# A four-layer vision tower on one core: runs of two to four unread matrix products taken out of the norms and the attentions

## The reference, cut to what matters

```python
h = tokens(x)
h = h + L0_attn(layernorm(h)); h = h + L0_ffn(layernorm(h))   # 16 heads, 16 experts, top 4
h = h + L1_attn(layernorm(h)); h = h + L1_ffn(layernorm(h))   # 2 heads, 8 experts, top 2
h = h + L2_attn(layernorm(h)); h = h + L2_ffn(layernorm(h))   # mla + a shared and 7 routed experts, top 2
h = h + L3_attn(layernorm(h)); h = h + L3_ffn(layernorm(h))   # attends across images; 8 experts, top 2
```

## Time and profile before

| what | us |
|---|---|
| runs: median, lowest, highest of 3 | 851.51, 849.39, 854.37 |
| the profiled execution's own time | 857.64 |
| its span, from the first to the last instruction | 855.5 |
| PE busy | 742.4 (87% of the span), 5946 records |
| DVE busy | 393.4 (46%) |
| POOL busy | 333.6 (39%) |
| ACT busy | 221.2 (26%) |
| mean share of the DMA engines' time, all queues | 44% |

### The profile page before, as it was taken

The page is one execution under the profiler, slowest core; times in us unless marked ns, Lnnn a source line. Parts: engine busy times, 40 slices in busy tenths (PEclk is TensorE's granted clock), DMA queues, the critical chain, the costliest instruction groups (busy, mean ns, idle before and its releaser), DMA issues. The chain is left out here.

```text
span 855.5 us, 16310 instructions
## 1 busy us (share of the span) xinstructions
PE 742.4 (87%) x5946; PEld 657.4 (77%) x5946; DVE 393.4 (46%) x1093; ACT 221.2 (26%) x588; POOL 333.6 (39%) x399
## 2 busy tenths in 40 slices
PE   6897898799999788899997897798999878879997
PEld 4785688688888677899986686577888754779996
DVE  3745967545433465411132864475431337532211
ACT  1021410254445032123201410142234025111120
POOL 2336541456664131244323423521354278243211
PEclk9897997899999999799998898798999988989999
DMA  9303005588885750787524101200486630255603
GB/s 366 162 7 49 8 2 176 182 246 236 241 239 160 246 178 1 265 269 233 180 76 98 13 2 38 22 3 31 113 270 191 271 52 11 69 198 215 233 17 101
DMA packets 79203, 116.94 MB, mean 137 GB/s; under 512 B 44566, under 2 KB 58071, under 8 KB 77207
## 3 DMA queue, kind: packets, MB, share of 16 engines
q1 hardware_dynamic: 66741, 88.46, 33.4%
q0 software_dynamic: 7968, 20.20, 7.9%
q10 hardware_dynamic: 4418, 7.25, 2.3%
HBM read 99.29 MB, written 16.60 MB: 135 GB/s over the span
## 5 line engine op out<-in xcount | busy, mean ns | idle before, releaser
L280 PE MATMUL ps<-const_sb 128*128 128x128 f32 x910 | 131.3, 303 | 0.0
L280 PEld LDWEIGHTS ps<-const_sb 128*128 128x128 f32 x910 | 124.6, 218 | 1.3 <-issue 0.5
L1840 PE MATMUL ps<-l0e_xg_fm,l0e_ring 128*128 128x128 f32 x544 | 72.7, 277 | 6.8 <-ACT l0e_up_sb L1924 3.1
L1840 PEld LDWEIGHTS ps<-l0e_xg_fm,l0e_ring 128*128 128x128 f32 x544 | 67.6, 191 | 12.8 <-issue 7.5
L922 PE MATMUL ps<-x_fm,w_sb 128*128 128x296 f32 x208 | 54.3, 413 | 0.0
L308 POOL TENSOR_TENSOR norm_r<-norm_ve,const_sb 128x2 f32<-128x2 f32 (+1 forms) x27 | 19.5, 724 | 88.3 <-DVE norm_ve L301 64.0
L1840 PE MATMUL ps<-l1e_xg_fm,l1e_ring 128*128 128x128 f32 (+1 forms) x408 | 50.8, 275 | 1.1 <-ACT l1e_xg_fm L1901 0.6
L1840 PEld LDWEIGHTS ps<-l1e_xg_fm,l1e_ring 128*128 128x128 f32 (+1 forms) x408 | 48.2, 182 | 2.5 <-issue 1.7
L1741 POOL DMA_INDIRECT l0e_y_scratch<-l0e_y_tm,l0e_rows_u x34 | 35.9, 1057 | 33.9 <-ACT l0e_y_tm L1948 29.9
L922 PEld LDWEIGHTS ps<-x_fm,w_sb 128*128 128x128 f32 x208 | 39.4, 190 | 11.8 <-DVE l1p_rot_b L953 0.3
L1726 POOL DMA_INDIRECT l0e_xg_tm<-x_scratch,l0e_rows_u x34 | 33.3, 980 | 22.1 <-PE ps L1804 9.3
(11 more groups left out here) (496 smaller groups left out, 1585.2 us busy)
## 6 DMA issues: line engine op xcount, KB each, us to landing
l0e_ring<-in_l_experts SPq DMA_DIRECT2D x34, 514.0 KB
l1e_ring<-in_l_experts SPq DMA_DIRECT2D x17, 704.0 KB
l2e_ring<-in_l_experts SPq DMA_DIRECT2D x16, 512.0 KB
expert_w<-in_l_experts SPq DMA_DIRECT2D x4, 2048.0 KB
l_more_w<-in_l_experts SPq DMA_DIRECT2D x4, 2048.0 KB
l0e_down_w<-in_l_experts SPq DMA_DIRECT2D x1, 4096.0 KB, 15.9
l1e_down_w<-in_l_experts SPq DMA_DIRECT2D x1, 3072.0 KB, 11.8
w_sb<-in_weights SPq DMA_DIRECT2D x2, 1032.0 KB, 6.8
```

The lines of the kernel that those rows point to most:

```text
L280: pe.matmul(ps[:, bank, 0:P], ident, ident, start=True, stop=True)
L1840: mm = pe.matmul(ps[0:widths[m], which, m * P:(m + 1) * P], w_n[:, c:c + widths[m]], x_n[:, k, :], start=(k == 0), stop=(k == KT - 1))
```

## The change

Seven of the calls of `stay_awake` are taken out, with the conditions around them. Nothing else is changed, and the thirteen others stay. Over the nine norms, three attentions of the common kind, the wide one and the one across images, 130 products go, which are 260 of the 1820 records on line 280 of matrix products and weight loads each counted singly for half of that: 910 matrix records before, 650 after.

```diff
--- before.py
+++ after.py
@@ -360,15 +360,12 @@
             def tensor(pe):
                 for t in range(TILES):
 
-                    if t in (2, 4):
-                        stay_awake(pe, 3)
                     pe.wait_ge(norm["normed"], TILES * n + t + 1)
                     for k in range(KT):
                         o = ps[:, 2 * k + t // 4, (t % 4) * P:(t % 4 + 1) * P]
                         mm = pe.transpose(o, dst[:, t, k * P:(k + 1) * P], ident)
                     if t >= 3:
                         mm.then_inc(norm["turned"], 1)
-                stay_awake(pe, 3, 4)
 
             def scalar(act):
                 for part, (c0, c1) in enumerate(((0, 512), (512, PADDED))):
@@ -798,8 +795,6 @@
                                 mm.then_inc(s_pt, 1)
                             if 0 <= n - 3:
                                 e = n - 3
-                                if n > pairs:
-                                    stay_awake(pe, 3)
                                 pe.wait_ge(s_ctx, e + 1)
                                 if e >= 1:
 
@@ -828,7 +823,6 @@
                                             v_bd[0:K3, 2 * e + s, b * REP:b * REP + nh, :]
                                             .rearrange("p h d -> p (h d)"), start=True, stop=True)
                                 mm.then_inc(s_av, 1)
-                        stay_awake(pe, 4)
 
                     @block.vector
                     def _(dve):
@@ -1249,8 +1243,6 @@
                             mm.then_inc(s_scores, 1)
 
                         for b in range(4):
-                            if b in (0, 2):
-                                stay_awake(pe, 3, 7)
                             pe.wait_ge(s_probs, b // 2 + 1)
                             for i in range(4):
                                 n = 4 * b + i
@@ -1465,8 +1457,6 @@
                                                        start=True, stop=True)
                                 mm.then_inc(s_scores, 1)
                             if has(n - 2):
-                                if isinstance(n, int) and n >= groups:
-                                    stay_awake(pe, 2, 2)
                                 pe.wait_ge(s_ctx, n - 1)
 
                                 pe.wait_ge(s_ctfm, n - 1)
@@ -1494,7 +1484,6 @@
                                             start=True, stop=True)
                                 mm.then_inc(s_av, 1)
                         pipeline(pe, groups, 2, step, first=8)
-                        stay_awake(pe, 4, 2)
 
                     @block.vector
                     def _(dve):
```

## The result

The changed kernel takes 862.30 us (median of 4 runs, 859.82 to 864.01), the kernel before 850.80 us (849.39 to 854.37, 4 runs), 11.5 us less. The ratio is 1.0121, with a 95% interval of 1.0071 to 1.0171, so the change makes the kernel slower. The forecast was 861.2 us, +9.7 us. The profiled execution took 864.01 us with a span of 862.0; the time is 6.4 us more than that of the profiled execution of before.

A forecast was written before the change was run, and what follows sets the result against it. PE's 87% busy share was no bound by itself; what counted was what unread products delay and do to the clock. Losses 20.2 + 3.4 less gains 13.9 made +9.7 us, added to the 851.51 us median: 861.2 us, range 854 to 868.

The forecast's parts named there:

- The case that I gave 0.66: Whole kernel: slower by +4.3 to +15 us, because low-clock losses exceed the gains; chance 0.66.
- per norm: Blocks behind the nine norms: 4.5 us at half speed each, losing 2.25 us; 20.2 us together, ends 12.6 and 27.9.
- the 6 that I had named as a sign: First projections behind a norm: line 911's 20 records take 6 to 8 us where the low clock reaches them.
- PE on the path at the start of all nine: Blocks behind the norms: all nine begin with the block waiting for PE, so low-clock time there is paid.
- The gains: Tails of norms and attention ends: work comes earlier without the runs, 1.0 + 6.1 + 4.4 + 2.4 = 13.9 us.
- The attentions: Output projections behind four attention ends: half of 1.7 us lost at each, 3.4 us together, ends 0 and 6.8.
- the four ends: Ends of the attentions: the last unread products delay the end; without them 0.6 us gained each, 2.4 us together.
- The faster one: Whole kernel: filling never held the clock, so the 13.9 us are gained, 837.6 us; chance 0.09.
- Short low stretches: Blocks behind norms: low for 3.4 us at most, loss meets gain, -1.3 to +4 us, some 852.5 us; chance 0.14.
- the rule of under 1% for ramps: Whole kernel: the skill's ramp penalty under 1% of span, 8.6 us; with the gain, -5.3 us or better.

The follow-up runs named there:

- p3: Kernel before with only the four runs at the attentions' ends, four products each, taken out: 849.42 us, ratio 0.9982 (0.9950 to 1.0014) to the kernel before.
- n2: Kernel before with only the attentions' runs out (44 products), all the norms' runs kept: 838.20 us, ratio 1.0111 to the kernel before (831.45 us).
- n1: Kernel before with only the nine norms' runs out (81 products), the attentions' kept: 846.65 us, ratio 1.0209 to the kernel before (831.45 us).
- p1: Changed kernel with more unread products added ahead of each norm's first transpose: 859.57 us, ratio 1.0120 to the kernel before (852.62 us).
- o4: Kernel before with only the three products ahead of tile 2 left in each norm: 839.87 us, ratio 1.0108 to the kernel before (831.13 us).
- o3: Kernel before with more products ahead of the norms and, inside each, only the run ahead of tile 2: 831.43 us, ratio 0.9977 to the kernel before.
- n3: Kernel before with only each norm's third run out (27 products, ahead of the barrier): 833.08 us, ratio 1.0025 to the kernel before (831.45 us).
- p2: Kernel before with more products ahead of the norms and longer kept runs in the routing: 843.84 us, ratio 0.9934 to the kernel before (852.62 us).
- o2: Kernel before with more unread products ahead of each norm's first transpose, all short runs kept: 831.34 us, ratio 0.9980 to the kernel before (831.13 us).

## Why the prediction was right, and where it was not

**The sign and the size** came out as forecast: +11.5 us in the medians against +9.7, and 862.3 lies 1.1 us from 861.2. The case that I gave 0.66 is the one that happened. That it came as close as 1.1 us is luck: the two profiles are 6.4 us apart, the medians of the second chip 14.8, and the sum holds errors on both sides, which follow.

**The step "per norm"** holds nearly to the number where it can be read alone. I had 4.5 us at half speed in each next block and 2.25 us lost. The four projection blocks have 3.1, 5.3, 5.0 and 5.0 us at 0.50, mean 4.6, and got longer by 1.51, 2.59, 1.36 and 2.42 us, mean 2.0. Line 905's 20 records took 7.02 and 6.97 us in layers 2 and 3, as in layer 1 more than the 6 that I had named as a sign. The total time at 0.50 rose by 51 us against 47. In the expert blocks it varies more, between -1.8 and +3.1 us, since the norm at their end and the low stretches that they had before fall in the same block. Over the nine it was 13.5 us in this one profile and not 20.2, but that is net of what three norms in the expert blocks gained. One block shows a step that was wrong: I had PE on the path at the start of all nine. The latents' eight records took 4.29 us against 2.23, yet the block got only 0.6 us longer with 4.4 us at 0.50, because before the change GpSimd's copy (line 668, until 524.74) ended that block 1.9 us after PE's last product (522.85).

**The gains** were over-priced. I had 13.9 us in the tails of norms and attentions. Where a norm had been low in its second half, 1.7 was right (1.9 measured in layer 1). Where it had been at the full clock it was 0.25 and not 0.5, as the fall now comes inside the norm; the six transposes behind 744.58 took 1.54 us, all at the low pace of the earlier trace rows. For the two norms that were low throughout I had 2.2 each; their blocks got shorter by 1.0 and 0.6 us. Gains and losses were both too large, so that their errors took from each other. The medians moved by 11.5, the two profiled executions by 6.4: that of before, 857.64 us, was slower than all four runs of its kernel. One pair of profiles could not have told whether the errors cancelled or not.

**The attentions** are the term whose reason fell. "The runs ahead of the waits for `s_ctx` end when VectorE's tile does, so they are costed at nothing" is about delay alone. I forgot there that such a run also carries the clock, the very thing that the rest of the sum is about. The price itself, +3.4 us in the output projections with ends of 0 and 6.8, was near: in the changed kernel layer 0's took 7.58 us and `mla`'s 6.24 against 4.56, which is 4.7 us, and the other two none.

```profile
116.79 7.58 PE L1052 MATMUL ps<-w_sb,l_ctx_fm 128*128 128x256 f32 x20 [0.64 <-PEq L707]
```

The 2.4 us that I had gained at the four ends can't be seen in p3, whose interval holds no change. n2's +1.1% for a term that I had at +1 us didn't show in the whole, as n1 and n2 overlap by 1.5%.

**The rivals.** The faster one needed a loss of under 0.7 us at each place; the four projections alone lost 2.0 each. "Short low stretches" needed 3.4 us at most behind each norm; one of the four projection blocks was so. The trace also speaks against the rule of under 1% for ramps (the Trainium skill, page "TensorE: Matmul & The Clock Gate", section "Part 1: The HAM clock gate"): the nine blocks behind a norm alone got 13.5 us longer, 1.6% of the span, with 47 of the 51 us more at 0.50, and the 116 us at 0.50 before the change come on top.

**On transposes** the trace agrees in a second place with what the earlier trace rows showed: six in 1.54 us at 0.50 in layer 3's norm, four in 0.76 at 1.00 (line 366 in layer 1's norm, at 342.16). The sentence of the Trainium skill (the same page, section "Part 4: PE-mode transpose") that the full clock doesn't engage for them isn't borne out for their pace, but they gain less than a product does: record by record they start 0.16 us apart at 1.00 and 0.21 at 0.50, the unread products 0.11 and 0.21. No run here shows by itself whether they count as work for the clock.

## What to carry to other kernels

Filling on TensorE has two prices, and both are read from the timeline: what it delays (is there a real instruction or a barrier right behind it?) and what stands behind it at which clock. Judge a short run not by its place but by the first 5 us of the next dense block, and test it by pairs. Here neither filling ahead of a norm (p1, without the attentions' runs) nor three products in its middle (o4) sufficed alone; together (o3) they did, with a third of the norms' short runs and 78 more products ahead. Of two runs ahead of the same block one can be enough: the attentions' last runs could go as long as the inner ones stayed. Where there is idle time ahead of a list of products, a longer run can end as the operands arrive; how much that gives by itself wasn't shown here, and one product too many is a delay.

## What the runs showed of the hardware that I had not expected

The kernel before took 831 us on the chips of the first two groups of experiments, 853 on the third's and 851 on the one of the first measurement. The clock accounts for little of it: its mean was 0.941 in both of the first two groups and 0.936 in the third, which is worth some 4 of the 22 us. Most of it is in the expert blocks: with only the norms' third runs out (n3), layer 0's takes 153.88 us on one of the faster chips, against 161.39 for the kernel before on the last, and all four are 17.6 us shorter of the 21.6 between the two spans. The projections of layers 0, 1 and 3 agree to 0.03 us where they are at 1.00. What in the expert blocks is faster wasn't tried.

The time of a run moves with its own clock: runs of the kernel before on one chip spread from 825.0 to 839.7 us. Of the five kernels within 0.7% of the one before that had twelve runs each, these told one (p2) from it and not the other four (n3, o2, o3, p3).
